# Attention value products of a graph layer: two heads of each graph put in the two halves of the partitions, one order of issue changed, the store split in two

## The chip, the cores and the metric

The kernel runs on one core of a Trainium2 chip. The metric is the time of one execution on the device, in microseconds (us). TensorE is the matmul engine (PE in the profile, its weight loads PEld), VectorE is DVE, ScalarE is ACT, GpSimd is POOL, SyncE is SP and here only issues DMAs.

## What is computed

Two graph attention layers, each followed by a residual and a layer norm, on 128 graphs of 64 nodes with 768 features. The change touches the first of them alone (its tensors are called L0 in the kernel). Cut to what matters:

```python
h = jnp.einsum('bnd,ade->bane', x, W)                  # 12 heads of 64
th = jnp.tanh(h)
attn = attn_src(th) + swap(attn_dst(th))               # 64 x 64 for each graph and head
attn = leaky_relu(attn); attn = jnp.where(adj, attn, -999.0)
attn = jax.nn.softmax(attn, axis=-1)
feat_out = jnp.einsum('banm,bame->bane', attn, h) + b  # the value products
feat_out = jax.nn.elu(heads_side_by_side(feat_out))
gate = jax.nn.sigmoid(x @ H_w.T + H_b)
x = layernorm(x + gate * feat_out + (1 - gate) * x)    # this mix and norm run in the second stage
```

The second layer is ordinary masked attention with 6 heads of 128 and four 768 x 768 projections.

## The kernel before

**Tiles.** The 8192 rows (128 graphs x 64 nodes) are cut into 64 tiles of 128 rows, two graphs each: graph 0 on partitions 0 to 63, graph 1 on 64 to 127. `layer0` makes `feat` and `gate` for all tiles and stores them in DRAM; then `layer1` loads all its weights, reads `feat` and `gate` back, and does the second layer in 32 groups of two tiles.

**Order of the work in `layer0`.** Each engine runs its own program; they meet through semaphores. A program is a list of steps T = 0 to 65, and one step holds stages of three tiles. On TensorE a step is: `project(0)` of tile T (line 424; 18 matmuls of 512 columns: 6 blocks of the contraction, each as high x high, high x low and low x high of operands split in two), the transposes of x of tile T+1 (line 411), `project(1)` of tile T, the value products of tile T-2 (line 459), `project(2)` of tile T (the gate), and the transposes of the softmax of tile T-1 (line 469). Before `project(0)` it waits for VectorE's copy of `h` of the tile before (`h_copied`, line 436 waits, line 389 copies).

**The value products.** For each of 12 heads and each of the two graphs there is one fp32 matmul with contraction over the 64 nodes of the graph. The stationary operand is `probsT[graph(g), a, :]` (64 x 64), the moving one `h_one[graph(g), u % 2, a, :]` (64 x 65: 64 features and a one that gives the row sum). `graph(g)` is partitions 64g to 64g+63. Both operands of graph g are on its half of the partitions, so the matmul uses its half of the array's rows; the result's partitions say which half of the array's columns it uses. Before, the result of graph g goes to partitions `graph(g)` of `ps_pv`, heads 0 to 5 in the first of its two PSUM banks and heads 6 to 11 in the second. So graph 0 uses one 64 x 64 quarter of the array and graph 1 the one diagonally opposite. `ps_pv` has 2 banks, partitions 0 to 127 of each.

**After them.** VectorE takes the reciprocals of the sums and scales (lines 380 and 382, `att`), ScalarE and VectorE do the ELU (lines 320, 322 and 401, `feat`), and SP stores `feat` (line 243). The addition that starts the logits (line 348) waits for `dst_all`, which goes through DRAM: line 376 makes `dst`, SP stores it (236), waits for that, and reads it back spread over the partitions (239). SP's program in a step is: gate of T-1 (226), x and adjacency of T+2 (230, 231), dst (236, 239), feat of T-2 (243). ScalarE's step begins with the softmax transposes' copies (285), then the gate (290, 292), mask, the copy of x transposed (269), tanh of h (309), exp (314), ELU (320, 322).

Of the kernel before, what the change touches and what calls it, by code (L numbers as in the profile page):

```python
# [18 lines left out]
HEADS0, E0 = 12, 64  # L19
# [98 lines left out]
def layer0(nc, x, adj, W, b, w_src, w_dst, Ht, H_b, feat_rows, gate_rows, dst_rows):  # L118

    NT = x.shape[0] // P  # L120
    x_t = x.rearrange("(t p) d -> t p d", p=P)
    adj_t = adj.rearrange("(t p) m -> t p m", p=P)
    feat_t = feat_rows.rearrange("(t p) d -> t p d", p=P)
    gate_t = gate_rows.rearrange("(t p) d -> t p d", p=P)
    HB = HEADS0 // 2
    EW = E0 + 1
    BLK = 512

    with ExitStack() as ctx:
# [14 lines left out]
        h_one = sb("h_one", [P, 2, HEADS0, EW])  # L144
# [10 lines left out]
        probsT = sb("probsT", [P, HEADS0, NODES])  # L155
        att = sb("att", [P, D])
        feat = sb("feat", [P, 2, D])
# [50 lines left out]
        def landed(T, u, slots):  # L208

            return (T - u % slots) * (16 // slots) + 16  # L210

        def graph(g):
            return slice(g * NODES, (g + 1) * NODES)

        @block.sync
        def _(sp):
            for t in range(2):
                sp.dma_start(x_tok[:, t, :], x_t[t]).then_inc(x_in[t], 16)
                sp.dma_start(adj_u8[:, t, :], adj_t[t]).then_inc(adj_in[t], 16)
            w_load(sp)  # L220

            def step(T, u, has):
                if has(-1):
                    slot = (u + 1) % 2
                    sp.wait_ge(gate_done, 2 * T)
                    sp.dma_start(gate_t[T - 1], gate[:, slot, :]).then_inc(gate_stored[slot], 16)
                if has(2):
                    sp.wait_ge(xT_done, T + 1)
                    sp.wait_ge(mask_done, T + 1)
                    sp.dma_start(x_tok[:, u % 2, :], x_t[T + 2]).then_inc(x_in[u % 2], 16)  # L230
                    sp.dma_start(adj_u8[:, (u + 2) % 4, :], adj_t[T + 2]).then_inc(adj_in[(u + 2) % 4], 16)
                if has(0):
                    sp.wait_ge(dst_done, T + 1)
                    if has(-1):
                        sp.wait_ge(sum_done, T)
                    sp.dma_start(dst_rows[u % 2].rearrange("(p a) -> p a", p=P), dst[:, :]).then_inc(dst_stored, 16)
                    sp.wait_ge(dst_stored, 16 * (T + 1))
                    for g in range(2):
                        sp.dma_start(dst_all[graph(g), :],
                                     dst_rows[u % 2][g * D:(g + 1) * D].partition_broadcast(NODES)).then_inc(dst_in, 16)  # L240
                if has(-2):
                    sp.wait_ge(elu_done, T - 1)
                    sp.dma_start(feat_t[T - 2], feat[:, u % 2, :]).then_inc(feat_stored[u % 2], 16)

            steps(sp, step, NT + 2)
            for s in range(2):
                sp.wait_ge(feat_stored[s], 16 * (NT // 2))
                sp.wait_ge(gate_stored[s], 16 * (NT // 2))

        @block.gpsimd  # L250
# [15 lines left out]
        @block.scalar  # L266
        def _(act):
            def transposed_hi(u):
                act.copy(xT_hi[:, u % 2, :, :].rearrange("p (b c) n -> p b (c n)", b=2),
                         banks(ps_t)).then_inc(hi_done, 1)  # L270

            act.wait_ge(xT_done, 1)
            transposed_hi(0)
            w_split_hi(act)

            def step(T, u, has):
                if has(-2):
                    act.wait_ge(pt_done, T - 1)
                    if has(-3):
                        act.wait_ge(pv_done, T - 2)  # L280
                    for parity in range(2):
                        for g in range(2):
                            out = probsT[graph(g), :, :].rearrange("p (b c two) n -> p b c two n", b=2, two=2)
                            pair = banks(ps_t)[graph(parity), :, :].rearrange("p b (c n) -> p b c n", c=KC // 2)
                            ins = act.copy(out[:, :, :, parity, :], pair[:, :, :, graph(g)])
                    ins.then_inc(ptc_done, 1)
                if has(-1):
                    g = gate[:, (u + 1) % 2, :]
                    act.wait_ge(z_done, T)
                    act.activation(g, g, ACT.Tanh, scale=0.5).then_inc(gate_done, 1)  # L290
                    act.wait_ge(gate_done, 2 * T - 1)
                    act.activation(g, g, ACT.Copy, scale=0.5, bias=0.5).then_inc(gate_done, 1)
                if has(0):
                    act.wait_ge(adj_in[u], landed(T, u, 4))
                    if has(-2):
                        act.wait_ge(masked_done, T - 1)
                    act.activation(not_adj[:, u % 2, :], adj_u8[:, u, :], ACT.Copy, scale=-1.0,
                                   bias=1.0).then_inc(mask_done, 1)
                if has(1):
                    act.wait_ge(xT_done, T + 2)  # L300
                    if has(-1):
                        act.wait_ge(g_done, T)
                    transposed_hi(u + 1)
                if has(0):
                    act.wait_ge(h_done, T + 1)
                    if has(-1):
                        act.wait_ge(thdst_done, T)
                        act.wait_ge(thsrc_done, T)
                    act.activation(th[:, :], ps_hg[:, 0:D], ACT.Tanh).then_inc(tanh_done, 1)
                if has(-1):  # L310
                    act.wait_ge(shift_done, T)
                    if has(-2):
                        act.wait_ge(pt_done, T - 1)
                    act.activation(probs[:, :], logits[:, :], ACT.Exp).then_inc(exp_done, 1)
                if has(-2):
                    act.wait_ge(att_done, T - 1)
                    if has(-4):
                        act.wait_ge(feat_stored[u % 2], landed(T - 4, u, 2))
                    f = feat[:, u % 2, :]
                    act.activation(f, att[:, :], ACT.Relu, scale=-1.0, bias=-1.0).then_inc(relu_done, 1)  # L320
                    act.wait_ge(relu_done, T - 1)
                    act.activation(f, f, ACT.Exp, scale=-1.0).then_inc(eexp_done, 1)

            steps(act, step, NT + 2)
# [82 lines left out]
        def _(pe):  # L407
# [23 lines left out]
            def step(T, u, has):  # L431
                first = isinstance(T, int) and T == 0
                if has(0):
                    pe.wait_ge(lo_done, T + 1)
                    if has(-1):
                        pe.wait_ge(h_copied, T)
                    project(0, u, first)
                if has(1):
                    if has(-2):
                        pe.wait_ge(ptc_done, T - 1)  # L440
                    transpose_x(T + 1, u + 1)
                if has(0):
                    if has(-1):
                        pe.wait_ge(z_done, T)
                    if has(-3):
                        pe.wait_ge(att_done, T - 2)
                    if has(-2):
                        pe.wait_ge(ptc_done, T - 1)
                    project(1, u, first).then_inc(h_done, 1)
                if has(-2):  # L450
                    pe.wait_ge(ident_ok, 1)
                    if not has(0):
                        pe.wait_ge(ptc_done, T - 1)
                        if has(-3):
                            pe.wait_ge(att_done, T - 2)
                    for a in range(HEADS0):
                        at = (a % HB) * EW
                        for g in range(2):
                            ins = pe.matmul(ps_pv[graph(g), a // HB, at:at + EW], probsT[graph(g), a, :],
                                            h_one[graph(g), u % 2, a, :], start=True, stop=True)  # L460
                    ins.then_inc(pv_done, 1)
                if has(0):
                    project(2, u, first).then_inc(g_done, 1)
                if has(-1):
                    pe.wait_ge(exp_done, T)
                    if has(1):
                        pe.wait_ge(lo_done, T + 2)
                    for c in range(KC):
                        ins = pe.transpose(banks(ps_t)[:, c // 3, (c % 3) * P:(c % 3 + 1) * P],
                                           probs[:, c * P:(c + 1) * P], ident[:, :])  # L470
                    ins.then_inc(pt_done, 1)
# [563 lines left out]
```

## Time and profile before

| what | us |
|---|---|
| median of 3 runs | 2995.43 (2994.34 to 2996.4) |
| the profiled execution, its own time | 2993.85 |
| span of that execution, first to last instruction | 2992.1 |
| TensorE busy | 2876.0 (96%) |
| TensorE weight loads busy | 2654.9 (89%) |
| VectorE busy | 1720.1 (57%) |
| ScalarE busy | 1061.4 (35%) |
| first layer, from the start to its last store's issue | about 1037 |

Busy time is the union of the engine's instructions. A matmul in the profile lasts from its start to the end of its results, so matmuls that follow closely overlap in it; the rate of a stream is read from starts, not from durations. An fp32 matmul with ordinary operands stands in the profile as two passes, each with its own weight load (64 tiles x 24 value products are 1536 matmuls and 3072 rows of each kind).

### The profile page before, as it was taken

The page shows a single profiled execution, that of the slowest core. Times are in us where ns is not written, and L with a number is a line of the kernel's source. Part 1 is how long each engine was busy: PE and PEld are TensorE (multiplying, and loading weights), DVE is VectorE, ACT ScalarE, POOL GpSimd, SP SyncE. Part 2 cuts the span into 40 slices and gives each one's busy share as a digit, 9 for nine tenths or more (in the row PEclk, how much of TensorE's full clock was granted, in tenths as well). Part 3 has the DMA queues.
Part 4 walks back from the last instruction along what each step waited for, and adds up shares of the span by engine and source line. Part 5 has one row for each costly group of instructions (what it writes and reads, how often), then busy time and mean ns, then how long its engine had stood idle before and what let it go on. Part 6 is the DMA issues. An engine that isn't in the chain of part 4 may idle for free.

```text
span 2992.1 us, 55247 instructions
## 1 busy us (share of the span) xinstructions
PE 2876.0 (96%) x21696; PEld 2654.9 (89%) x21696; DVE 1720.1 (57%) x3335; ACT 1061.4 (35%) x2597; POOL 471.6 (16%) x265
## 2 busy tenths in 40 slices
PE   7999999999999619999999999999999999999998
PEld 6888888888888519999999999999999999999998
DVE  6888888888888644444444444444444444444443
ACT  4554445445454423322232232233223222322332
POOL 0111111110111011111211211121111112111110
PEclk9999999999999859999999999999999999999999
DMA  4332332233323241111111211111121111111110
GB/s 149 103 99 99 103 106 98 98 101 106 106 95 101 101 159 54 54 44 65 65 43 45 75 54 44 65 56 52 44 66 63 43 55 64 54 44 65 64 33 22
DMA packets 107364, 221.15 MB, mean 74 GB/s; under 512 B 36544, under 2 KB 36544, under 8 KB 107200
## 3 DMA queue, kind: packets, MB, share of 16 engines
q1 hardware_dynamic: 107200, 218.58, 21.9%
q8 instruction: 149, 2.44, 0.3%
q14 instruction: 15, 0.12, 0.0%
HBM read 142.65 MB, written 75.89 MB: 73 GB/s over the span
## 4 chain that ended last, share of the span: by engine, by line
PE 62%; DMA 1%; DVE 1%; issue 0%; POOL 0%; ACT 0%; SPq 0%; DVEq 0%; POOLq 0%
PE L_ps_k L108 14%; PE L_ps_q L108 14%; PE L_ps_a L108 14%; PE L_ps_a L957 14%; PE L_ps_s L920 2%; PE L_ps_c L940 2%; PE L_ps_pt L940 1%; PE L_ps_pt L927 1%; PE L_ps_q L871 0%; PE L_ps_s L871 0%; PE L_ps_k L871 0%; DMA L_gate<-gate_scratch 0%; DMA L_x_tok<-Wf 0%; DMA L_x_tok<-Wk 0%; DVE L_w_lo L97 0%
## 5 line engine op out<-in xcount | busy, mean ns | idle before, releaser
L424 PE MATMUL L_ps_hg<-L_w_hi,L_xT_hi 128*128 128x512 f32 x1152 | 474.0, 411 | 11.7 <-DVE L_w_lo L97 11.4
L424 PE MATMUL L_ps_hg<-L_w_hi,L_xT_lo 128*128 128x512 f32 x1152 | 455.9, 396 | 0.0
L424 PE MATMUL L_ps_hg<-L_w_lo,L_xT_hi 128*128 128x512 f32 x1152 | 455.9, 396 | 0.0
L108 PE MATMUL L_ps_q<-L_xT_hi,L_w_hi 128*128 128x256 f32 x1152 | 328.2, 285 | 7.4 <-issue 6.0
L108 PE MATMUL L_ps_k<-L_xT_hi,L_w_hi 128*128 128x256 f32 x1152 | 332.5, 289 | 0.0
L108 PE MATMUL L_ps_q<-L_xT_lo,L_w_hi 128*128 128x256 f32 x1152 | 326.7, 284 | 0.0
L108 PE MATMUL L_ps_q<-L_xT_hi,L_w_lo 128*128 128x256 f32 x1152 | 326.6, 284 | 0.0
L108 PE MATMUL L_ps_k<-L_xT_hi,L_w_lo 128*128 128x256 f32 x1152 | 325.8, 283 | 0.0
L108 PE MATMUL L_ps_k<-L_xT_lo,L_w_hi 128*128 128x256 f32 x1152 | 325.6, 283 | 0.0
L657 ACT ACTIVATE L_qT<-L_ps_q,L_bq_col 128x256 f32<-128x256 f32 x192 | 80.5, 470 | 687.9 <-PE L_ps_q L108 687.9
L424 PEld LDWEIGHTS L_ps_hg<-L_w_hi,L_xT_hi 128*128 128x128 f32 x1152 | 217.3, 189 | 61.2 <-DVE L_w_lo L97 9.2
L619 POOL TENSOR_TENSOR L_feat<-L_feat,L_x_tok 128x768 f32<-128x768 f32 x64 | 117.5, 1835 | 967.0 <-DMA L_x_tok<-x 730.0
L957 PE MATMUL L_ps_a<-L_w_hi,L_cT_hi 128*128 128x384 f32 x768 | 264.2, 344 | 0.0
L424 PEld LDWEIGHTS L_ps_hg<-L_w_hi,L_xT_lo 128*128 128x128 f32 x1152 | 217.6, 189 | 51.7
L108 PE MATMUL L_ps_a<-L_w_hi,L_xT_hi 128*128 128x384 f32 x768 | 263.0, 342 | 0.0
L957 PE MATMUL L_ps_a<-L_w_hi,L_cT_lo 128*128 128x384 f32 x768 | 258.1, 336 | 0.0
L957 PE MATMUL L_ps_a<-L_w_lo,L_cT_hi 128*128 128x384 f32 x768 | 258.1, 336 | 0.0
L108 PE MATMUL L_ps_a<-L_w_hi,L_xT_lo 128*128 128x384 f32 x768 | 256.8, 334 | 0.0
L108 PE MATMUL L_ps_a<-L_w_lo,L_xT_hi 128*128 128x384 f32 x768 | 256.8, 334 | 0.0
L262 POOL TENSOR_TENSOR L_th_src<-L_th,L_wsrc_all 128x768 f32<-128x768 f32 x64 | 118.4, 1851 | 875.8 <-DVE L_th_dst L372 875.8
L424 PEld LDWEIGHTS L_ps_hg<-L_w_lo,L_xT_hi 128*128 128x128 f32 x1152 | 218.3, 190 | 42.6
L108 PEld LDWEIGHTS L_ps_q<-L_xT_hi,L_w_hi 128*128 128x128 f32 x1152 | 221.8, 192 | 11.9 <-issue 10.1
(110 smaller groups left out, 5939.6 us busy)
## 6 DMA issues: line engine op xcount, KB each, us to landing
L_x_tok<-x SPq DMA_DIRECT2D x64, 384.0 KB, 3.3
L_dst_all<-dst_scratch SPq DMA_DIRECT2D x128, 192.0 KB, 3.3
gate_scratch<-L_gate SPq DMA_DIRECT2D x64, 384.0 KB, 2.5
feat_scratch<-L_feat SPq DMA_DIRECT2D x64, 384.0 KB, 2.3
L_x_tok<-x SPq DMA_DIRECT2D x32, 768.0 KB, 4.3
L_feat<-feat_scratch SPq DMA_DIRECT2D x64, 384.0 KB, 3.1
L_gate<-gate_scratch SPq DMA_DIRECT2D x64, 384.0 KB, 3.6
out<-L_x_tok SPq DMA_DIRECT2D x32, 768.0 KB, 3.5
```

What stands on the lines that cost most here:

```text
L108: ins = pe.matmul(out, left[a][c], right[b][c], start=(n == 0), stop=(n == len(terms) - 1))
L262: pool.tensor_tensor(th_src[:, :], th[:, :], wsrc_all[:, :], ALU.mult).then_inc(thsrc_done, 1)
L424: ins = pe.matmul(ps_hg[:, cols], xT[a][c], w[bb][c], start=(c == 0 and n == 0), stop=(c == KC - 1 and n == 2))
L619: pool.tensor_tensor(feat[:, :], feat[:, :], x_tok[:, s, t], ALU.subtract).then_inc(delta_done, 1)
L657: act.activation(dst[h], ps[:, h * GN:(h + 1) * GN], ACT.Identity, bias=col[:, a:a + 1]).then_inc(signal, 1)
L920: ins = pe.matmul(ps_s[g * NODES:(g + 1) * NODES, k * NODES:(k + 1) * NODES], qT[:, j % 2, h, n], kT[:, h, n], start=True, stop=True)
L927: ins = pe.transpose(ps_pt[:, h * P:(h + 1) * P], probs[:, h * GT:(h + 1) * GT, :].rearrange("p t m -> p (t m)"), ident[:, :])
L940: ins = pe.matmul(ps_ctx[j][:, h * GN + t * P:h * GN + (t + 1) * P], v_tok[:, t, a * E1:(a + 1) * E1], probsT[:, (s + j) % 2, h * GT + t, ...
L957: ins = pe.matmul(ps_a[o_bank[n]][:, 0:HALF], left[a][c], right[b][c], start=(c == 0 and k == 0), stop=(c == KC - 1 and k == 2))
```

## The change

The loop over the value products is turned. Head `a = half * 6 + k` of graph g now gives its result to partitions `graph(half)`, bank g. So the four matmuls issued one after another (two halves for each of two graphs) use the four quarters of the array: rows by graph, columns by half. The number, shapes and operands of the matmuls are the same; VectorE and ScalarE run the same instructions on the same shapes. Row `half * 64 + n` of `att` and `feat` now holds node n of both graphs, six heads of each. The store puts the halves of a row together: two DMAs in place of one, each from 64 partitions with two pieces of 384 numbers (1,536 bytes) for each partition, in place of one DMA of 3,072 bytes for each of 128 partitions. The semaphore `feat_stored` therefore counts 32 for a tile in place of 16.

```diff
@@ SP's step
                     sp.wait_ge(elu_done, T - 1)
-                    sp.dma_start(feat_t[T - 2], feat[:, u % 2, :]).then_inc(feat_stored[u % 2], 16)
+                    rows = feat_t[T - 2].rearrange("(g n) (half f) -> half n g f", g=2, half=2)
+                    for half in range(2):
+                        sp.dma_start(rows[half], feat[graph(half), u % 2, :].rearrange("n (g f) -> n g f", g=2)).then_inc(
+                            feat_stored[u % 2], 16)
@@ SP's end
-                sp.wait_ge(feat_stored[s], 16 * (NT // 2))
+                sp.wait_ge(feat_stored[s], 32 * (NT // 2))
@@ ScalarE's step, before the ELU
-                        act.wait_ge(feat_stored[u % 2], landed(T - 4, u, 2))
+                        act.wait_ge(feat_stored[u % 2], 2 * landed(T - 4, u, 2))
@@ TensorE's step, the value products
-                    for a in range(HEADS0):
-                        at = (a % HB) * EW
+                    for k in range(HB):
                         for g in range(2):
-                            ins = pe.matmul(ps_pv[graph(g), a // HB, at:at + EW], probsT[graph(g), a, :],
-                                            h_one[graph(g), u % 2, a, :], start=True, stop=True)
+                            for half in range(2):
+                                a = half * HB + k
+                                ins = pe.matmul(ps_pv[graph(half), g, k * EW:(k + 1) * EW], probsT[graph(g), a, :],
+                                                h_one[graph(g), u % 2, a, :], start=True, stop=True)
                     ins.then_inc(pv_done, 1)
```

## Rows read from the trace of the kernel before

**Rows 1.** Busy time of each engine in a stretch, with instructions, granted clock, DMA share

```profile
core 0: us, PE busy (x) PEld busy (x) DVE busy (x) ACT busy (x) POOL busy (x), PEclk, DMA share, GB/s
58.00:1011.00 953.00, 953.00 (x6949) 779.17 (x6948) 791.62 (x856) 473.55 (x731) 112.88 (x61) 1.00 0.31 101
```

**Rows 2.** Groups by line of TensorE between 58 and 1011 us

```profile
L424 PE MATMUL L_ps_hg<-L_w_hi,L_xT_hi 128*128 128x512 f32 x1098 | 450.2, 410 | 0.0
...
L459 PE MATMUL L_ps_pv<-L_h_one,L_probsT 64*64 64x65 f32 x2928 | 98.6, 219 | 0.0
```

**Rows 3.** Timeline of one step, all engines: start us, us, instruction, [idle before it <-releaser]

```profile
605.30 1.62 PE L459 MATMUL L_ps_pv<-L_h_one,L_probsT 64*64 64x65 f32 x48
605.41 0.81 ACT L309 ACTIVATE L_th<-L_ps_hg 128x768 f32<-128x768 f32 x1 [3.38 <-PE L_ps_hg L424]
606.25 0.96 DVE L372 TENSOR_TENSOR L_th_dst<-L_th,L_wdst_all 128x768 f32<-128x768 f32 x1 [1.30 <-ACT L_th L309]
...
606.85 0.50 PE L424 MATMUL L_ps_hg<-L_w_hi,L_xT_hi 128*128 128x512 f32 x1
...
609.34 0.95 DVE L389 TENSOR_TENSOR L_h_one<-L_ps_hg,L_b_less 128x768 f32<-128x768 f32 x1
...
611.74 0.48 PE L424 MATMUL L_ps_hg<-L_w_hi,L_xT_hi 128*128 128x512 f32 x1
...
613.21 0.36 SPq L243 DMA_DIRECT2D feat_scratch<-L_feat  x1
613.89 1.58 DVE L348 TENSOR_TENSOR L_logits<-L_dst_all,L_src 128x768 f32<-128x768 f32 x1 [0.70 <-DMA L_dst_all<-dst_scratch]
...
619.54 0.95 DVE L329 TENSOR_TENSOR L_xT_lo<-L_ps_t,L_xT_hi 128x768 fp32r<-128x768 f32 x1
...
620.94 1.62 PE L459 MATMUL L_ps_pv<-L_h_one,L_probsT 64*64 64x65 f32 x48
```

**Rows 4.** Line 459 alone, in stretches of 20 to 30 ns: (x) counts what is under way

```profile
605.30:605.32 0.02, 0.01 (x2) 0.02 (x2) 1.00 0.00 0
...
605.35:605.38 0.03, 0.03 (x2) 0.03 (x4) 1.00 0.00 0
...
605.40:605.43 0.03, 0.03 (x4) 0.03 (x6) 1.00 0.00 0
...
605.46:605.49 0.03, 0.03 (x6) 0.03 (x6) 1.00 0.00 0
```

**Rows 5.** The same view, columns PE, PEld, clock, DMA, of the last burst

```profile
1030.20:1030.25 0.05, 0.01 (x2) 0.04 (x2) 0.50 0.76 307
...
1030.36:1030.39 0.03, 0.03 (x3) 0.03 (x5) 0.50 0.49 198
1030.39:1030.42 0.03, 0.03 (x4) 0.03 (x5) 0.50 1.81 717
...
1030.47:1030.50 0.03, 0.03 (x5) 0.03 (x5) 0.50 0.77 307
1030.50:1030.53 0.03, 0.03 (x6) 0.03 (x5) 0.50 0.78 307
```

**Rows 6.** Timeline of TensorE, small fp32 matmuls of the second layer

```profile
1534.79 0.69 PE L920 MATMUL L_ps_s<-L_kT,L_qT 128*64 128x64 f32 x16
...
1559.88 1.05 PE L940 MATMUL L_ps_c<-L_probsT,L_v_tok 128*128 128x128 f32 x8
```

**Rows 7.** Timeline of all engines at the end of the first layer

```profile
1019.86 2.86 PE L459 MATMUL L_ps_pv<-L_h_one,L_probsT 64*64 64x65 f32 x48 [2.06 <-issue]
...
1025.22 0.22 DVE L380 RECIPROCAL L_row_inv<-L_ps_pv 128x12 f32<-128x12 f32 x1
...
1030.24 2.86 PE L459 MATMUL L_ps_pv<-L_h_one,L_probsT 64*64 64x65 f32 x48 [2.87 <-issue]
1033.14 0.23 DVE L380 RECIPROCAL L_row_inv<-L_ps_pv 128x12 f32<-128x12 f32 x1 [3.96 <-PE L_ps_pv L459]
```

**Rows 8.** The page's DMA issues: count, KB each, median us to landing

```profile
L_dst_all<-dst_scratch SPq DMA_DIRECT2D x128, 192.0 KB, 3.3
...
feat_scratch<-L_feat SPq DMA_DIRECT2D x64, 384.0 KB, 2.3
```

**Rows 9.** Durations (ns min/median/max) over the whole span, by source line

```profile
L459 PE MATMUL L_ps_pv<-L_h_one,L_probsT x3072: 216/218/365, 58.2 to 1032.8; 64*64 64x65 f32 x192
...
L920 PE MATMUL L_ps_s<-L_kT,L_qT x1536: 222/222/271, 1126.4 to 2956.4; 128*64 128x64 f32 x192
...
L940 PE MATMUL L_ps_c<-L_probsT,L_v_tok x512: 272/275/348, 1151.5 to 2968.9; 128*128 128x128 f32 x171
```

## The prediction

> **What bounds the kernel now.** I read first the busy times by stretch, then the groups by line, then the timeline of one step, then the changed line alone in stretches of tens of nanoseconds. Between 58 and 1011 us TensorE is busy in all of 953.00 us at full clock, VectorE in 791.62 and ScalarE in 473.55 [rows 1]. The reader is to see that the first layer is a stream of matmuls without a gap, so what comes off that stream comes off the time, as long as no other engine becomes late. Nearly all of the stream is the three projections; the changed line is 2,928 passes of the 61 steps between those bounds [rows 2]. A step is 15.64 us, from 605.30 to 620.94, and its value products hold TensorE from 605.30 to the next projection at 606.85, 1.55 us or 10% of it [rows 3]. The second layer, two thirds of the span, is not touched.
>
> **How fast the changed line runs now.** The burst is 48 passes. From first start to last end it takes 1.62 us [rows 3], and one pass lasts 218 ns [rows 9], so first start to last start is 1.40 us. The passes start in pairs: at 605.40 to 605.43 two more are under way than before, at 605.46 to 605.49 two more again [rows 4]. The second pair starts some 107 ns after the first, because of its weights; the other 22 intervals are (1.40 - 0.107) / 22 = 58.6 ns. What does a pass cost by itself? A full-array fp32 matmul of 128 columns has 8 passes in 1.05 us, one lasting 0.275, so (1.05 - 0.275) / 7 = 111 ns for each [rows 6, 9]. For 65 columns this scales to 56 ns. So a pair takes what one pass takes: the two quarters already run side by side, and the bound is one quarter's own stream of passes, 24 in a burst. The other bound that would give the same rate is issue, 29 ns for each pass with its weight load.
>
> **Which of the two it is** decides the forecast. In the last burst the clock is at the lower level, 0.50. There, a third pass appears at 1030.36 to .39, a fourth at .39 to .42, a fifth at .47 to .50, a sixth at .50 to .53 [rows 5]: two streams, each with a pass about every 108 ns, one about 33 ns behind the other. Scaled by the clock, one pass of 65 columns is 2 x 56 = 112 ns. So the streams are limited by the array, each is never idle, and the stagger with which they began remains. If issue were the limit, it would not have doubled just so. How far does the engine look ahead? The two passes of one fp32 matmul need the same quarter, and I take them to be issued together. Yet a second weight load starts within the first 20 ns of the burst, and two more after 50 [rows 4]. A load that must wait for the quarter could not start so early, so the first two are of different quarters: the second matmul went past the waiting second pass of the first. That is a look-ahead past one matmul. With four quarters it must go past three; no row shows that.
>
> **The change, part by part.**
> *Value products, 61 bursts.* Count, shape and operands stay; they are spread over four quarters, 12 passes in each. With every quarter streaming by itself, a burst has 12 rounds: 0.107 + 10 x 0.0586 + 3 x 0.007 for the stagger of four = 0.71 us from first to last start, against 1.40. That is 0.69 saved. The issue that this needs is four passes with their loads in 58 ns; the last burst issued the second tile's load 36 ns or less after the first tile's [rows 5], with one full matmul (two loads, two passes) between them, so 9 ns an instruction from an empty queue. 96 instructions take 0.86 us at that rate, 0.15 over 0.71; but before a burst the queue has had a 4 us projection in which to fill. I take no loss; without that cover it would be 61 x 0.15 = 9 us. Bounds: nothing saved (the look-ahead ends after one matmul) and 0.69.
> *Two quarters with the same rows.* The second layer's scores use all rows and two column halves: 16 passes of 64 columns in 0.69 us, one lasting 0.222, that is (0.69 - 0.222 - 0.107) / 6 = 60 ns a pair [rows 6, 9]. So sharing rows costs nothing. Sharing the columns, where graph 0 and graph 1 write the same partitions of two banks at once, is shown by no row.
> The Trainium skill ("TensorE: Matmul & The Clock Gate", Part 3, The mechanism) says that matmuls keep strict order in start and end, and that a weight load overlaps a matmul only when its row group differs. By the first, the second passes of each matmul would block the next two quarters and nothing would be saved; by the second, column halves with the same rows could not overlap. Rows 4 speak against the first and rows 6 against the second.
> *What must keep up.* `project(0)` waits for `h_one`: line 389 ends at 610.29, TensorE wants it at 611.74 [rows 3]. It hangs on the end of `project(1)`, before the burst, so its slack falls from 1.45 to 0.76 us. VectorE's cycle from line 372 to the end of 329 is 606.25 to 620.49, 14.24 us, with 0.70 in it of waiting for `dst_all` [rows 3]; the step becomes 14.95, and the tanh that line 372 waits for comes that much sooner, so its wait of 1.30 falls to about 0.6. Neither turns into a stall. If VectorE did become the bound, no step could be under about 14.3 us.
> *The reciprocal, scaling, ELU:* same instructions on the same shapes; nothing.
> *The store.* One DMA issue more, 0.36 us of SP [rows 3], at the end of SP's step where it next waits for the gate; before `dst_all` is next issued most of a step passes. Its pieces are half as long. The landing lies between that of one 384 KB store, 2.3 us, and of a 192 KB load from the scratch, 3.3 [rows 8], and nobody waits for it for two steps. It is hidden 63 times by SP's waiting; without that cover it would cost at most 63 x 0.36 = 23 us. After the last tile the layer's end waits for it: between 0.36 (issue) and 1.4 us (issue and 1.0 of landing); I take 0.4, as the halves are smaller.
> *The ends.* The burst that begins at 1011.12 and that at 1019.86 are off the path: after the second, VectorE takes up line 380 only at 1025.22 [rows 7], 2.5 us after its end at 1022.72. The last, at 1030.24, is on it: 380 starts right at its end. It takes 2.86 - 0.31 = 2.55 from first to last start at about 108 ns a pair; 12 rounds fewer, less 0.07 for the stagger, save 1.2 us.
> *Sum:* 61 x 0.69 + 1.2 - 0.4 = 42.9 us. Against the profiled execution, 2993.85 - 42.9 = 2951.0; its own time is 1.6 under the median of the runs, so the median should become 2995.4 - 42.9 = 2952.5.
>
> **The rivals.**
> *A. Four at a time, 60%.* For it: rows 4 to 6. 2952.5, with its own range 2946 to 2962.
> *B. Part of it, 14%.* The look-ahead or the issue keeps only three quarters going: 16 rounds in place of 12, so 8 x 58.6 = 0.47 saved a burst, 28.7 + 0.8 - 0.4 = 29: 2966. Up to 2985 if less.
> *C. The change doesn't do what it says, 18%.* The engine looks past one matmul only; or passes begin in program order, so that the second pass of each matmul holds back the next quarter, and only neighbours in that order overlap; or the two quarters that write the same partitions take turns. Each way two quarters run at a time, as now. 0 + 0.4: 2996. For it: nothing before shows more than two at once.
> The Trainium skill ("TensorEngine Tiling (Array Packing)", Gotcha 1) has it that row tiles may not use one PSUM bank at the same time; no row here shows it, as now both graphs write one bank in pairs at full rate [rows 4], which speaks against it, and after the change they write different banks.
> *D. Slower, 8%.* Each quarter shares rows with one neighbour and columns with another. If neighbours exclude each other and the look-ahead doesn't reach the diagonal one, passes go one by one: 48 x 56 = 2.69 against 1.40, 61 x 1.29 = +79: 3075. It is slower as soon as a burst takes over 1.40 from first to last start, that is over 29 ns a pass. Against it: the scores share rows at full rate [rows 6].
>
> **How the numbers follow.** A measurement of this kernel can tell about 0.2%, 6 us, from no change. A and B make it faster: 0.74, less a little for a weak B, 0.73. Same is C and that rest: 0.19. Slower is D: 0.08. The prediction is A's, 2952.5. The range must take in C, whose sign is the other one, to leave out no more than 2 in 10: 2946 (A with all 1.55 us of a burst halved, 47 us, and some 2 of spread between runs) to 2998 (C with 1.4 us for the last store, and spread). Left out is D.
>
> **What would show it.** In the profile after: the burst at 0.93 us in place of 1.62 from first start to last end; counts under way that grow by four in 58 ns; a step of 14.95 us; VectorE's wait before line 372 near 0.6 with no new wait of TensorE before `project(0)`; two stores a tile, 128 of 192 KB. Wrong would be: the burst still at 1.62 (C), between (B), over (D); or a burst at 0.93 but a step that is not shorter, with TensorE waiting for `h_one` or for the softmax, which would mean that the slacks were misread.

## The result and the profile after

The changed kernel takes 2949.66 us (median of 4 runs, 2949.18 to 2950.46) against 2995.61 before (4 runs): ratio 0.9847, 95% interval 0.983 to 0.9864. The span of the profiled execution fell from 2992.1 to 2948.3 us, by 43.8. Forecast were 2952.5, in a range from 2946 to 2998, and 42.9 less.

The stretches, as in [rows 1]: us, then busy time and instructions of PE, PEld, DVE, ACT and POOL, granted clock, DMA share, GB/s:

```profile
59.00:969.00 910.00, 910.00 (x6946) 737.23 (x6936) 784.19 (x855) 473.07 (x731) 112.88 (x61) 1.00 0.37 106
```

The same 61 steps are in it. TensorE is still busy in all of it, and the stretch is 43 us shorter. One step, all engines, against [rows 3]:

```profile
611.31 0.93 PE L463 MATMUL L_ps_pv<-L_h_one,L_probsT 64*64 64x65 f32 x48
611.41 0.81 ACT L312 ACTIVATE L_th<-L_ps_hg 128x768 f32<-128x768 f32 x1 [3.38 <-PE L_ps_hg L427]
612.17 0.50 PE L427 MATMUL L_ps_hg<-L_w_hi,L_xT_hi 128*128 128x512 f32 x1
...
612.26 0.96 DVE L375 TENSOR_TENSOR L_th_dst<-L_th,L_wdst_all 128x768 f32<-128x768 f32 x1 [0.39 <-ACT L_th L312]
...
615.35 0.95 DVE L392 TENSOR_TENSOR L_h_one<-L_ps_hg,L_b_less 128x768 f32<-128x768 f32 x1
...
617.03 0.47 PE L427 MATMUL L_ps_hg<-L_w_hi,L_xT_hi 128*128 128x512 f32 x1
...
618.91 1.50 SPq L245 DMA_DIRECT2D feat_scratch<-L_feat  x2
619.67 1.58 DVE L351 TENSOR_TENSOR L_logits<-L_dst_all,L_src 128x768 f32<-128x768 f32 x1 [0.79 <-DMA L_dst_all<-dst_scratch]
...
626.23 0.93 PE L463 MATMUL L_ps_pv<-L_h_one,L_probsT 64*64 64x65 f32 x48
```

The burst of 48 passes takes 0.93 us from first start to last end, where it took 1.62. The next projection starts 0.86 us after the burst's start, where it was 1.55. The step is 14.92 us here (626.23 - 611.31) and 14.95 in every other one, 14.93 on average, in place of 15.63. VectorE's wait for tanh is down from 1.30 to 0.39, and `project(0)` at 617.03 finds `h_one` ready at 616.30: its slack fell from 1.45 to 0.73.

The changed line alone, in stretches of 20 to 40 ns, PE (x) and PEld (x) counting what is under way, against [rows 4]:

```profile
611.30:611.34 0.04, 0.03 (x4) 0.03 (x4) 1.00 0.00 0
611.35:611.39 0.04, 0.04 (x4) 0.04 (x8) 1.00 0.00 0
611.42:611.44 0.02, 0.02 (x8) 0.02 (x12) 1.00 0.00 0
611.46:611.50 0.04, 0.04 (x12) 0.04 (x12) 1.00 0.00 0
```

Four weight loads are under way within 40 ns. Four more passes are there in the third stretch and four more again in the fourth, 58 ns apart by their starts. That is the pattern of [rows 4] with four for two.

The end of the first layer, all engines, against [rows 7]:

```profile
977.09 0.93 PE L463 MATMUL L_ps_pv<-L_h_one,L_probsT 64*64 64x65 f32 x48 [2.06 <-issue]
...
982.88 0.22 DVE L383 RECIPROCAL L_row_inv<-L_ps_pv 128x12 f32<-128x12 f32 x1
...
987.89 1.58 PE L463 MATMUL L_ps_pv<-L_h_one,L_probsT 64*64 64x65 f32 x48 [2.46 <-issue]
989.53 0.23 DVE L383 RECIPROCAL L_row_inv<-L_ps_pv 128x12 f32<-128x12 f32 x1 [2.70 <-PE L_ps_pv L463]
```

The last burst, at the lower clock, is 1.58 in place of 2.86. Its start has moved from 1030.24 to 987.89, by 42.35 us. From there to the end of the span it was 1961.86 us and is 1960.41: 1.45 less, of which the burst itself is 1.28.

The 42.35 come from three places. The 61 steps take 42.62 less (0.70 each). The last tile's trip of `dst` through DRAM, off TensorE, happens to be 0.28 shorter. The first burst starts 0.55 later (58.72 against 58.17).

What follows the last burst holds a cost too. Lines of SP, before and after:

```profile
1037.13 0.33 SPq L243 DMA_DIRECT2D feat_scratch<-L_feat  x1
1039.99 6.16 SPq L87 DMA_DIRECT2D L_x_tok<-Wq  x6
```

```profile
993.52 1.25 SPq L245 DMA_DIRECT2D feat_scratch<-L_feat  x2
997.40 6.26 SPq L87 DMA_DIRECT2D L_x_tok<-Wq  x6
```

From the last tile's store to the second layer's first load it was 2.86 us and is 3.88: the split store costs 1.02 us here, once. From that load to the end it is 1.2 us shorter, in code that is the same; that part takes 1950.3 to 1953.9 us in the nine traces of this case that have all value products, so 1.2 is within what it varies by.

The page's DMA issues, against [rows 8]:

```profile
L_dst_all<-dst_scratch SPq DMA_DIRECT2D x128, 192.0 KB, 3.3
...
feat_scratch<-L_feat SPq DMA_DIRECT2D x128, 192.0 KB, 2.7
```

A half of the store lands after 2.7 us, where the whole took 2.3. In the steps nothing waits for it; at the layer's end the 1.02 us above do.

### The profile page after: what moved, and what is told of

Its sections match the earlier page's. It is cut to its first block, busy times and chain, and to the rows that moved or that the text cites. A ratio compares the mean times of both kernels' runs of the same rounds, so it can differ in the third digit from the quotient of the medians.

```text
span 2948.3 us, 55423 instructions
## 1 busy us (share of the span) xinstructions
PE 2828.1 (96%) x21696; PEld 2608.0 (88%) x21696; DVE 1709.5 (58%) x3335; ACT 1061.2 (36%) x2597; POOL 471.4 (16%) x265
## 4 chain that ended last, share of the span: by engine, by line
PE 63%; DMA 1%; DVE 1%; issue 0%; POOL 0%; ACT 0%; SPq 0%; DVEq 0%; POOLq 0%
PE L_ps_k L108 14%; PE L_ps_q L108 14%; PE L_ps_a L108 14%; PE L_ps_a L961 14%; PE L_ps_s L924 2%; PE L_ps_c L944 2%; PE L_ps_pt L944 1%; PE L_ps_pt L931 1%; PE L_ps_q L875 0%; PE L_ps_s L875 0%; PE L_ps_k L875 0%; DMA L_gate<-gate_scratch 0%; DMA L_x_tok<-Wf 0%; DMA L_x_tok<-Wk 0%; DVE L_w_lo L97 0%
```

## The experiments

Three questions were left. How far does TensorE look ahead, as the forecast hung on it? Did the store give anything back? And what holds the step now? In all of them "burst" is the time from first start to last start of the 48 passes: the timeline's figure less the 0.22 us of one pass.

**Other orders of the same 24 matmuls.** Four kernels issue exactly the changed kernel's matmuls, with the same operands and results, and differ in the loops alone (runs_of_two is shortened here by the line that takes `g` and `half` out of `gh`):

```diff
 changed kernel
                     for k in range(HB):
                         for g in range(2):
                             for half in range(2):
 half_outer
+                    for half in range(2):
+                        for k in range(HB):
+                            for g in range(2):
 graph_outer
+                    for g in range(2):
+                        for k in range(HB):
+                            for half in range(2):
 quarter_major
+                    for g in range(2):
+                        for half in range(2):
+                            for k in range(HB):
 runs_of_two
+                    for k0 in range(0, HB, 2):
+                        for gh in range(4):                 # g, half = gh // 2, gh % 2
+                            for k in range(k0, k0 + 2):
```

*half_outer.* 

> The same 24 value products and results as the changed kernel, ordered half, head, graph: the first 12 matmuls alternate between the two quarters of column half 0 (graph 0, graph 1), the last 12 between those of column half 1. Theory 'near' (TensorE looks past a few waiting matmuls, enough for the three that the changed order needs): only two quarters run at a time, which write the same partitions of two banks; the burst takes 1.40 us from first to last start as before the change, the step 15.6, the time 2992. Theory 'far' (whatever is queued for an idle quarter starts): the second half's quarters start in the first 50 ns too, burst 0.71, time 2950. Theory 'columns conflict' (two row groups that write the same partitions take turns): 48 passes of 56 ns, 2.7 us, time 3072; the changed kernel then owes its gain to row neighbours and diagonals alone.

*graph_outer.* 

> The same matmuls ordered graph, head, half: the first 12 alternate between the two column halves of graph 0's rows, the last 12 between those of graph 1's. 'Near': 1.40 us, time 2992, equal to the half-outer order. 'Far': 0.71 us, 2950. If sharing rows costs something that sharing columns doesn't, this order is the slower of the two.

*quarter_major.* 

> The same matmuls ordered graph, half, head: six in a row for each quarter. 'Near': quarters overlap only where one run of six ends and the next begins; up to 48 x 56 ns = 2.7 us from first to last start, time about 3070. 'Far': 0.71 us, 2950. A middle reach gives a middle time, and the start of the second quarter's first weight load tells the reach directly: it must pass 22 or so waiting instructions.

*runs_of_two.* 

> The same matmuls, the changed order with two heads in a row for each quarter. To start the fourth quarter TensorE must look past six matmuls in place of three. 'Near' with a reach of three or four matmuls: two quarters at a time, burst 1.4 us, time 2992. 'Far': 0.71 us, 2950.

In this set the kernel before took 2994.22 us. Half_outer took 2982.63 (ratio 0.9959, 0.9943 to 0.9974), graph_outer 2981.7 (0.9959, 0.9943 to 0.9975), quarter_major 3047.65 (1.0181, 1.0151 to 1.021), runs_of_two 2957.33 (0.9879, 0.985 to 0.9908). The bursts in TensorE's timelines, half_outer and graph_outer first, then quarter_major, then runs_of_two:

```profile
521.38 1.45 PE L463 MATMUL L_ps_pv<-L_h_one,L_probsT 64*64 64x65 f32 x48
```

```profile
521.22 1.45 PE L463 MATMUL L_ps_pv<-L_h_one,L_probsT 64*64 64x65 f32 x48
```

```profile
519.82 2.48 PE L463 MATMUL L_ps_pv<-L_h_one,L_probsT 64*64 64x65 f32 x48
```

```profile
511.67 1.03 PE L464 MATMUL L_ps_pv<-L_h_one,L_probsT 64*64 64x65 f32 x48
```

That is 1.23 for both of the first two, 2.26 and 0.81 us (0.82 by the starts themselves). Neither "near" (1.40 and 2.7) nor "far" (0.71) is right: there is a reach, and it is of middle length. "Columns conflict" has fallen: in half_outer two quarters that write the same partitions run side by side at 58 ns a pair, and graph_outer, whose pairs share rows, comes out the same. So neither neighbour costs anything. The same matmuls in the order quarter_major are slower than the kernel before (3047 and 3049 us against 2991 to 2995), though they use four quarters.

Where does the second quarter start in quarter_major? Counts under way of that burst:

```profile
520.23:520.26 0.03, 0.03 (x4) 0.03 (x3) 1.00 0.00 0
520.29:520.31 0.02, 0.02 (x4) 0.02 (x3) 1.00 0.00 0
520.35:520.37 0.02, 0.02 (x5) 0.02 (x4) 1.00 0.00 0
520.40:520.42 0.02, 0.02 (x5) 0.02 (x5) 1.00 0.00 0
520.46:520.48 0.02, 0.02 (x6) 0.02 (x6) 1.00 0.00 0
520.57:520.60 0.03, 0.03 (x7) 0.03 (x4) 1.00 0.00 0
```

A single stream keeps four passes under way (218 ns each, one started every 58). It does so up to 520.31; from 520.33 on a second one runs along. The single starts in the trace are eight, at 519.816 to 520.276; the ninth, at 520.331, has the second quarter's first only 6 ns behind it. The first quarter has 12 passes, so three were still waiting when issue got past them. In half_outer the third and fourth quarters begin at 521.914 and 521.920, just behind the ninth pass of each of the first two: three waiting again, in each, six in all.

So the reach isn't one number of passes for the whole engine. Issue had got past three waiting passes in quarter_major and six in half_outer; in runs_of_two all four quarters have begun by 40 ns, before the second pass of any, which is nine.

This gives a theory with one number: **each quarter holds three waiting passes beside the running one; issue is in program order and stands still when the next pass's quarter is full.** I counted it through for all orders with 58.5 ns a pass, and tested it on an order not used to find it. Every matmul here is two passes, so room for four passes and room for two matmuls give the same counts; no run tells them apart.

*runs_of_three.* The loop of runs_of_two with three heads in place of two (`k0` in steps of 3). 

> The changed order with three heads in a row for each quarter, six passes. Theory 'three wait': each quarter holds at most three waiting passes beside the running one, and issue, in program order, stands still when the next pass's quarter is full. By a count with 58.5 ns a pass that gives 1.40, 0.71, 1.23, 2.27 and 0.86 us for the orders before, changed, half-outer, quarter-major and runs of two (measured 1.40, 0.71, 1.23, 2.26, 0.82), and 1.56 us for this one: time 2950 + 61 x 0.85 = 3001, slower than the kernel before although all four quarters are used. 'Four wait' gives 1.15 us and 2976, 'five wait' 0.86 and 2959; 'far' reach 0.71 and 2950.

```profile
530.97 1.76 PE L464 MATMUL L_ps_pv<-L_h_one,L_probsT 64*64 64x65 f32 x48
```

The burst is 1.54 us, the time 3002.26 against 2993.61 before (ratio 1.0027, 1.0015 to 1.0039). "Three wait" gave 1.56 us and 3001; "four wait" 1.15 and 2976. The starts show the rule at work: the second quarter's first pass comes 172 ns into the burst, 6 ns behind the first quarter's third pass, when three of its six were still waiting.

| order | burst by "three wait" | measured | time |
|---|---|---|---|
| before (two quarters) | 1.40 | 1.40 | 2993.6 |
| changed | 0.71 | 0.71 | 2951.3 |
| half_outer | 1.23 | 1.23 | 2982.6 |
| quarter_major | 2.27 | 2.26 | 3047.7 |
| runs_of_two | 0.86 | 0.81 | 2957.3 |
| runs_of_three | 1.56 | 1.54 | 3002.3 |

(The first two times are those of the second set.) The one that is off is runs_of_two, by 0.05. A count made after the runs takes two more times from the starts: 6.7 ns to issue one matmul, and 107 ns in place of 58.5 to a pass that wasn't yet waiting when its quarter began the one before. With three waiting it gives 0.83 for runs_of_two, where a quarter's second run of passes is held up in just this way, and 1.40, 0.71, 1.23, 2.25 and 1.52 for the others. With four waiting it gives 1.17, 2.08 and 1.07 for half_outer, quarter_major and runs_of_three, so three stands. The times follow the bursts: 61 x (1.23 - 0.71) = 32 over the changed kernel is 2983 for half_outer, 61 x 1.55 = 95 is 3046 for quarter_major.

**The changed kernel again**, as the yardstick of the second set. 

> The changed kernel itself, as the yardstick of this set: 2950, burst 0.714 us from first to last start, step 14.93.

It took 2951.32 against 2993.61, ratio 0.986 (0.9843 to 0.9876): 42.3 us.

**The store alone.**

```diff
-                    sp.dma_start(feat_t[T - 2], feat[:, u % 2, :]).then_inc(feat_stored[u % 2], 16)
+                    rows = feat_t[T - 2].rearrange("p (half f) -> half p f", half=2)
+                    for half in range(2):
+                        sp.dma_start(rows[half], feat[:, u % 2, half * HALF:(half + 1) * HALF]).then_inc(
+                            feat_stored[u % 2], 16)
```

with the two waits on `feat_stored` doubled. 

> The kernel before with the store alone split: two DMAs a tile, one for each half of the columns, 1,536 bytes a piece as in the changed kernel. Theory 'hidden': step 15.63 as before, two issues that keep SP 0.85 us apart as in the changed kernel, at most 1 us at the end of the layer: 2994 to 2996, no difference to be measured. Rival 'the store costs what the burst gave': SP is late for the gate's store or dst, and the step grows by up to 0.3 us, 20 us in all.

It took 2993.76 us against 2993.61: ratio 1.000, 0.999 to 1.0009. TensorE's bursts stand 15.63 us apart. SP's timeline of it:

```profile
519.08 0.90 SPq L245 DMA_DIRECT2D feat_scratch<-L_feat  x2
521.91 0.33 SPq L226 DMA_DIRECT2D gate_scratch<-L_gate  x1
```

SP has done with both halves 1.93 us before it takes up the gate. In the steps the store is hidden. The expectation was wrong in a detail: the two issues together take 0.90 us here, in the changed kernel 1.50. So the store here isn't quite the changed kernel's. Its halves are cut another way: 128 partitions with one piece each here, 64 partitions with two pieces each there, at the same bytes and the same number of pieces. Which of the two, the partitions or the pieces in each, makes the difference isn't shown. It shows elsewhere too: a half lands after 1.9 us here and 2.7 there, and at the layer's end, from the store to the second layer's first load, it is 2.94 us here, 3.88 there and 2.86 before. It is this cut, and not the halving, that costs the 1 us there.

**What holds the step when the burst shrinks on.**

```diff
+                    full = isinstance(T, int) and T < 4
-                    for k in range(HB):
+                    for k in range(HB if full else 1):
```

> The changed kernel with one sixth of the value products: after the first two tiles only heads 0 and 6 are multiplied, four matmuls a tile, and the other heads' results are left from earlier tiles. It asks what holds the step when the burst goes on shrinking. Theory 'TensorE still': the burst is 0.107 + 0.02 + 0 = 0.13 us from first to last start, 0.58 less, the step 14.35, the time 2950 - 61 x 0.58 = 2915. Theory 'VectorE and the trip of dst through DRAM' (from line 375's start to the end of 332 took 14.0 to 14.5 us, then tanh): the step stops near 14.5 and the time near 2924, with TensorE waiting for h_one or lo_done.

It took 2917.76 us (ratio 0.9746, 0.9727 to 0.9766). VectorE's timeline, and the start of `project(0)` in the same step:

```profile
518.93 0.95 DVE L332 TENSOR_TENSOR L_xT_lo<-L_ps_t,L_xT_hi 128x768 fp32r<-128x768 f32 x1
519.80 0.95 DVE L375 TENSOR_TENSOR L_th_dst<-L_th,L_wdst_all 128x768 f32<-128x768 f32 x1
...
522.88 0.95 DVE L392 TENSOR_TENSOR L_h_one<-L_ps_hg,L_b_less 128x768 f32<-128x768 f32 x1
...
528.14 1.54 DVE L351 TENSOR_TENSOR L_logits<-L_dst_all,L_src 128x768 f32<-128x768 f32 x1 [1.72 <-DMA L_dst_all<-dst_scratch]
...
533.74 0.95 DVE L332 TENSOR_TENSOR L_xT_lo<-L_ps_t,L_xT_hi 128x768 fp32r<-128x768 f32 x1
```

```profile
523.16 0.82 PE L474 MATMUL L_ps_t<-L_ident,L_probs 128*128 128x128 f32 x6
523.97 0.47 PE L427 MATMUL L_ps_hg<-L_w_hi,L_xT_hi 128*128 128x512 f32 x1
```

The median step is 14.34 us, as "TensorE still" has it, and TensorE is busy in 748.86 of the 750 us from 100 to 850. But the mean step is 14.41, and the time is 2.8 us over the forecast 2915. `project(0)` starts 0.57 us after the transposes before it when nothing holds it. In the step shown it is 0.81, and it starts 0.14 us behind the end of `h_one`, at 523.83. That is so in 13 of the 58 steps after 100 us, 3.7 us in all; in the others it is ready just in time. VectorE now goes from one instruction to the next almost without the wait for tanh (13 waits, 3.7 us). From line 375's start to 332's end it takes 14.34 us on average, as much as the median step; 14.89 in the one shown, 13.9 to 15.2 in all.

So TensorE bounds the changed kernel, and about 0.6 us of its step of 14.93 could still come off. At 14.34 VectorE's chain, with the trip of `dst` in it, begins to hold the step.

## Why the prediction was right

- **TensorE's stream sets the first layer's time, and what comes off it comes off the whole.** Right: 0.69 us came off the burst and 0.70 off the step. In the other orders the step followed the burst within 0.02 us, up and down.
- **A quarter's own stream of passes is the bound, not issue.** Right. The forecast burst was 0.71 from first to last start; measured 0.71. Runs_of_three, quarter_major and the rest issue the same number of instructions and take up to three times as long. The prediction took 9 ns an instruction for the issue from an empty queue, and hoped that the projection before would cover it. That price was wrong. In the last burst after the change, again from an idle TensorE, the first loads of the four quarters start at 0, 36, 43 and 49 ns: the 36 ns stand once, and a further matmul, two loads and two passes, is issued in 6.7 ns.
- **The look-ahead reaches past three matmuls.** This was the step that no row of before could show, and the reason for rival C's 18%. It holds, but by another rule than the one I had in mind. The prediction spoke of a number of matmuls to look past; what the runs fit is room for three waiting passes in each quarter. In the changed order each quarter is given two passes at a time, so issue seldom meets a full one before the others have their work. The 0.52 us between this order and half_outer, and 1.55 to quarter_major, show how much hung on the order of the loops.
- **Rivals B, C and D.** Times between A's and C's, as B has them, and slower ones, as D has them, are met by other orders of the same matmuls: 2957 and 2982, 3002 and 3048. That the order tried was one of the good ones was not worked out beforehand, and is in part luck: the 60% for A rested on a reach that no row of before showed. D's mechanism, neighbours that exclude each other, isn't there. C's strict order of passes isn't either: in quarter_major, a pass of the second quarter starts at 520.337, ahead of three that the program has earlier.
- **Strict order, and loads of the same rows.** In quarter_major the starts are out of program order, and graph_outer's pairs, in the same rows, run at 58 ns a pair. The Trainium skill ("TensorE: Matmul & The Clock Gate", Part 3, The mechanism), in its list of what overlaps, has matmuls strictly in order and a weight load overlapping only with matmuls of another row group. The trace agrees with neither as they stand. The section's opening also allows a load into a background weight buffer; whether the loads here are such isn't shown. The same section's statement that tiles of the array work at once is borne out: four quarters halve the burst of two. The Trainium skill ("TensorEngine Tiling (Array Packing)", Gotcha 1) says that different row tiles can't use one PSUM bank at the same time. Before the change both graphs wrote one bank at once, on different partitions, at 58 ns a pair, so the trace doesn't agree there; the same partitions of one bank weren't tried.
- **Slacks.** `h_one`: 0.76 forecast, 0.73 found. VectorE's wait for tanh: about 0.6 forecast; 0.39 in the step shown, 35.6 us in 51 waits (0.70 each) between 100 and 900 us. From the end of `dst` to the addition that waits for it, 5.3 to 6.2 us pass, depending on the step, and this wait takes the difference up. That VectorE could follow down to about 14.3 us a step was right as well: in one_head, at 14.34, it begins to hold TensorE up.
- **The store.** Hidden, as forecast. One issue more of 0.36 us was wrong: SP is held 1.50 us in place of 0.36, three times the extra that I took. In the steps it cost nothing because SP's wait for the gate covers it. At the layer's end, where nothing covers it, the price was 1.02 us in place of the 0.4 put down. That is inside the bounds given there, 0.36 to 1.4, but the reason for the low end of them, that the halves are smaller, was wrong: each half lands later than the whole did, after 2.7 us against 2.3.
- **The sum.** 61 x 0.69 + 1.2 - 0.4 = 42.9 was forecast. The same three terms measure 42.6 + 1.3 - 1.0 = 42.9. That they agree so closely is luck: the steps gave 0.5 more and the store took 0.6 more. The spans differ by 43.8, the second set's medians by 42.3, the first's by 45.9; runs of one kernel lie up to 5.4 us apart. (In the working, (1.40 - 0.107) / 22 is 58.8 and not 58.6 ns; over ten rounds it changes the burst by 0.002 us.)

## What to carry to other kernels

Small matmuls that use different quarters of the array run side by side only if they are issued so that no quarter is given more than a few in a row. Here, with fp32 matmuls of two passes, one in a row gave the full rate (0.71 us), two cost 0.1 us a burst, three 0.83 and six 1.55. So rotate through the quarters with the innermost loops. Before costing such a change, look at a burst at the lower clock: if the starts keep their stagger and each stream takes twice as long, the array and not the issue sets the rate. Look at its first 50 ns as well: a second quarter's load that comes before the first quarter's passes are done shows that the streams are independent. Neither shows how far the engine gets ahead; that took kernels with other orders.

And look at what a change of layout does to the DMA behind it where nothing covers it, at the end of a stage and not only in the steps.

## What the runs showed of the hardware

- Each 64 x 64 quarter takes up to three waiting passes beside the running one, in fp32 matmuls of two passes each; the bursts of six orders of the same work (0.71 to 2.26 us) fit this within 0.05 us, one of them forecast.
- Issue is no bound there: the first passes of four quarters start 7 ns apart, with a matmul of two passes and two loads for each.
- Passes of later matmuls start before waiting passes of earlier ones when their quarter is free (quarter_major, 520.337).
- Two quarters that write the same partitions of two PSUM banks, and two that read the same partitions, run at the full rate of 58 ns a pass.
- Two stores of 192 KB from 64 partitions with two pieces of 1,536 bytes each hold SP for 1.50 us and land after 2.7; from 128 partitions with one such piece each it is 0.90 and 1.9.
